# A prologue's opening in another order, its ScalarE loop written out with one table load, and twenty instead of sixteen maximum pairs beside projections

## The reference

```python
x = x + attn(layernorm(x))        # x: 4096 x 256, 16 heads of 16
x = x + ffn_fp8(layernorm(x))     # 256 -> 256, quantised to fp8 values

# attn:
qkv = x @ Wqkv + b                                  # q, k, v by head
y_softmax = softmax(causal(q k^T / 4)) v
state = (1 - sigmoid(Lambda)) * state + Gamma * (v_t outer k_t / 4)   # per token
y_stp = (W_static + state) q_t
alpha = sigmoid(gelu(x @ gate_w1 + b1) @ gate_w2 + b2)
return (alpha * y_softmax + (1 - alpha) * y_stp) @ out_w + out_b
```

## Time and profile before

| | us |
|---|---|
| median of 3 runs (1756.3 to 1759.27) | 1756.9 |
| profiled execution | 1765.1 |
| its span | 1763.3 |
| TensorE busy | 1626.0 |
| VectorE busy | 1520.4 |
| ScalarE busy | 1394.1 |
| GpSimd busy | 1249.5 |

### The profile page before, as it was taken

How to read it: one execution, slowest core, us unless ns; L and a number is a source line. 1 busy time by engine, 2 the same in 40 slices (tenths; PEclk the granted TensorE clock), 3 DMA queues, 4 the chain that set the end, 5 groups by cost and what they waited for, 6 DMA issues and landing times. The chain is left out here.

```text
span 1763.3 us, 44702 instructions
## 1 busy us (share of the span) xinstructions
PE 1626.0 (92%) x17582; PEld 587.1 (33%) x17582; DVE 1520.4 (86%) x1736; ACT 1394.1 (79%) x2839; POOL 1249.5 (71%) x1159
## 2 busy tenths in 40 slices
PE   5996699999999999999999999999999999999655
PEld 3541133223333332333333322333333332333542
DVE  6568899999899999998999999989999999830778
ACT  3652388998987889989888998898888889898234
POOL 4435487778777777787777777877788888870645
PEclk9995599999999999999999999999999999999876
DMA  4885333241222331422124222322252221200702
GB/s 131 272 267 165 80 88 87 73 103 57 74 67 85 101 89 56 96 78 70 59 87 111 68 80 71 83 72 67 77 119 83 78 83 43 79 5 17 254 32 96
DMA packets 115346, 163.22 MB, mean 93 GB/s; under 512 B 30080, under 2 KB 57792, under 8 KB 115136
## 3 DMA queue, kind: packets, MB, share of 16 engines
q1 hardware_dynamic: 112608, 158.74, 30.7%
q10 hardware_dynamic: 2528, 1.64, 0.3%
HBM read 121.87 MB, written 38.01 MB: 91 GB/s over the span
## 5 line engine op out<-in xcount | busy, mean ns | idle before, releaser
L1519 DVE TENSOR_REDUCE pmax<-PS 128x2 f32<-128x1024 f32 (+2 forms) x1120 | 1204.2, 1130 | 85.3 <-PE PS L1318 67.2
L1472 ACT ACTIVATE probs<-PS 128x512 f32<-128x512 f32 (+3 forms) x2304 | 1149.1, 576 | 157.0 <-PE PS L1356 77.9
L1383 PE MATMUL PS<-probs,V_g 128*17 128x256 f32 (+3 forms) x5064 | 395.9, 385 | 4.1 <-ACT o_t L1493 3.7
L1226 POOL TENSOR_TENSOR v_exp<-v_exp,k_rows 128x512 f32<-128x512 f32 x256 | 321.9, 1283 | 28.1 <-DMA v_exp<-qkv_t 27.9
L1356 PE MATMUL PS<-Q_st,K_st 50*128 50x512 f16 (+3 forms) x1408 | 289.1, 365 | 7.9 <-ACT probs L1472 6.3
L1268 POOL TENSOR_TENSOR state<-odd,q_rows 128x514 f32<-128x514 f32 x256 | 281.7, 1132 | 6.1
L1318 PE MATMUL PS<-K_st,Q_st 48*128 48x512 f16 (+3 forms) x1408 | 272.9, 357 | 0.2
L1383 PE MATMUL PS<-probs,V_first 128*17 128x256 f32 (+2 forms) x3296 | 265.3, 394 | 2.2 <-ACT o_t L1493 2.2
L1356 PE MATMUL PS<-Q_st,K_first 50*128 50x512 f16 (+3 forms) x896 | 194.4, 380 | 11.0 <-ACT probs L1472 5.0
L1318 PE MATMUL PS<-K_first,Q_st 48*128 48x512 f16 (+1 forms) x832 | 179.1, 392 | 19.6 <-DVE pmax L1519 19.4
L1257 POOL COPY carry<-odd 128x4 f32<-128x4 f32 x64 | 12.0, 187 | 252.6 <-DVE odd L1554 252.6
(11 more groups left out here) (194 smaller groups left out, 1511.6 us busy)
## 6 DMA issues: line engine op xcount, KB each, us to landing
v_exp<-qkv_t SPq DMA_DIRECT2D x256, 256.0 KB
qkv_t<-proj SPq DMA_DIRECT2D x24, 512.0 KB, 4.1
qk_parts<-parts SPq DMA_DIRECT2D x16, 512.0 KB, 5.2
Q_st<-qk_parts SPq DMA_DIRECT2D x192, 32.0 KB, 3.8
v_rows<-vaug SPq DMA_DIRECT2D x8, 544.0 KB, 6.1
xin<-x SPq DMA_DIRECT2D x8, 512.0 KB, 6.5
k_rows<-qkv_t SPq DMA_DIRECT2D x16, 256.0 KB, 4.0
q_rows<-qkv_t SPq DMA_DIRECT2D x16, 256.0 KB, 6.1
```

Of the source, the lines that this page charges most:

```text
L1226: pool.tensor_tensor(v_exp[:, n % RING], v_exp[:, n % RING], k_rows[:, b % 2], ALU.mult)\
L1383: mm = pe.matmul(PS[h * VW:h * VW + VN, out_bank(g, s), first:end], v[:, kt, h * VN:(h + 1) * VN], probs[:, tile % P_SLOTS, h, first - r * ...
L1472: act.activation(probs[:, tile % P_SLOTS, h, 0:CH - r * P], PS[:, step[5], 0:CH - r * P], ACT.Exp, scale=SCORE_SCALE).then_inc(exp_done, 1)
L1519: dve.tensor_reduce(pmax[:, s % 2, pair * TPC + j:GH * TPC:PAIRS * TPC, blk], PS[:, bank:bank + SIDES, 0:width], AX.X, ALU.max).then_inc(m ...
```

## The change

It has five parts.

1. `PAIRS_AT`: chunk 5 keeps four pairs but starts one unit later, chunk 6 gets seven (six before), chunk 7 nine (six before). A unit may have two pairs behind it; `project` counts them.
2. The ten K_first fills of GpSimd move from behind the second `power` into its loop: four behind the third `power`, four behind the fourth, two behind the fifth.
3. ScalarE's loop is written out for all chunks, and a Gelu of one column stands after the weights. Its output is overwritten later.
4. VectorE's `low_columns(0, 0)` moves ahead of the last steps of the scales.
5. `set_recurrence` becomes three functions. `peak_of_ffn` stays ahead of the loop, `set_decays` (the eight steps up to `gains_ready`) goes behind `split(0, 0)`, `set_static` (`static_j`) behind `low_columns` of the same round.

```diff
-PAIRS_AT = {5: (2, 3, 4, 5), 6: (0, 1, 2, 3, 4, 5), 7: (0, 1, 2, 3, 4, 5)}
+PAIRS_AT = {5: (3, 4, 5, 5), 6: (0, 0, 1, 2, 3, 4, 5), 7: (0, 0, 1, 2, 2, 3, 4, 4, 5)}
...
                     power(2)
-                    for pair in range(PAIRS):
-                        for c in range(FIRST):
-                            pool.memset(K_first[:, pair, c * CH:(c + 1) * CH], SHIFT_UNIT).then_inc(shift_rows_ready, 1)
                     pool.wait_ge(pool_setup, 12)
...
                         power(c1)
+                        for c in range(2 * (c1 - 3), min(2 * (c1 - 2), FIRST)):
+                            for pair in range(PAIRS):
+                                pool.memset(K_first[:, pair, c * CH:(c + 1) * CH], SHIFT_UNIT).then_inc(shift_rows_ready, 1)
...
-                            if u in between:
+                            for _ in range(between.count(u)):
                                 first_maxima(MAX_BANKS[pairs_made % 2], 2 if pairs_made else 1)
...
+                    act.activation(gate_t[:, 0, 0:1], w1_sb[:, 0, 0:1], ACT.Gelu)
...
-                    with act.Fori(0, NCH // 2 - 1) as it:
+                    for it in range(NCH // 2 - 1):
...
                     low_weights(w_parts[:, 1, :, 0:2 * D], wqkv_sb[:, :, 0:2 * D], w_parts[:, 0, :, 0:2 * D], 1)
+                    low_columns(0, 0)
...
-                    low_columns(0, 0)
...
-                    set_recurrence()
+                    peak_of_ffn()
                     for it in range(NCH // 2 - 2):
                         for par in range(2):
                             split(it, par)
+                            if it == 0 and par == 0:
+                                set_decays()
                             low_columns(it + par, 1 - par)
+                            if it == 0 and par == 0:
+                                set_static()
```

More of the change, by code:

```diff
@@ L975, in link, with peak_of_ffn @@
                         dve.wait_ge(dve_setup, n_setup)
-                    def set_recurrence():
+                    def peak_of_ffn():
                         dve.wait_ge(weights_loaded, 16 * N_WEIGHTS)
@@ L983, in set_recurrence, with set_decays @@
                         dve.tensor_copy(ffn_peaks[:, :], wsmall[:, 0:1].broadcast_to([P, P])).then_inc(weights_peak, 1)
+                    def set_decays():
                         dve.wait_ge(act_setup, 1)
@@ L994, in set_recurrence, with set_static @@
                         dve.sem_inc(gains_ready, 1)
+                    def set_static():
                         n_c = HD // TPC
```

## The result

The change makes the kernel faster: median 1748.57 us (1745.2 to 1752.51) against 1757.3 us (1755.73 to 1764.23) of the kernel before, timed in turn; the ratio is 0.9948 with a 95% interval of 0.9937 to 0.996. That is 8.7 us, where 12.5 were forecast; 1748.6 lies inside the range, 4.2 us above the predicted 1744.4.

What follows compares the result with a forecast made beforehand. The prologue was taken to be clocked by TensorE's chunks, its gains passing on whole through block two. Steps 1 to 7 gave -10.0 us and step 8 -2.5, together -12.5 from the median 1756.9: 1744.4, range 1738.5 to 1751.

Steps and rivals of the forecast that it cites:

- block two passing it on whole: Second block, behind a barrier of all engines: whatever the first block gains or loses passes on whole.
- Step 1: Start of chunk 0: low_columns(0,0) ahead of the scales' six small instructions, -1.06 us; chunk 0 keeps its 10.62.
- Step 2: Gap before chunk 1: ten fills leave VectorE's way, chunk 1 starts near 33.6 instead of 39.44, -5.8 us including step 1.
- a clock that isn't regained: Rival: chunks 1 and 3 still begin at half clock, losing 2.4 + 1.7 us, giving 1748.5; chance 0.15.
- Step 3: Chunk 1: idle time gone, so it runs at full clock, 9.27 instead of 11.63 us, -2.4; running sum -8.2.
- Step 4: Before chunk 2: static_j held by low_half(0), then xn held by four fills, +1.0 us; running sum -7.0.
- Step 5: Gap into chunk 3: table load gone, -1.28 us, but VectorE's full round makes TensorE wait, +0.95; running sum -7.1.
- Step 6: Chunks 3 to 5: chunk 3 at full clock -1.7 us, gap 4 to 5 without table load -1.28; chunk 5 at -9.7.
- Step 7: K loads in chunk 5: first pair at 91.1 us after waiting some 1.2, one unit less behind; chunk 5 ends at -10.0.
- Step 8: Chunks 6, 7 and tail: four fewer pairs at the end -4.2 us, their cost beside the chunks +1.75; net -2.5.
- transfers crowd: Rival: chunk 3's stores land 3 us late and the K gate is late by as much, giving 1747.5; chance 0.05.

Runs made afterwards that it cites:

- after: Profiled execution of the whole changed kernel, against the kernel before: span 1746.1 us against 1763.3.
- p_gate_unit3: Block one of the changed kernel alone, chunk 5's pairs placed as in the change but sixteen pairs in all: median 162.0 us (160.8 to 163.77).
- the block alone: Block one of the changed kernel, blocks two and three left out: median 159.75 us, against 166.83 and 171.76 for the two groups of block one of before.
- p_idle_fills: Block one of the changed kernel alone, five fills ahead of the third power and five ahead of the sixth: median 158.2 us, against the change's 159.75.
- after_again: The whole changed kernel once more, unchanged, in another session: 1749.13 us (1747.26 to 1752.72), ratio to before 0.9958.
- one-fill block: Block one of the kernel before alone, its ten K_first fills written as one instruction: 171.37 to 172.69 us in six runs.

## Why the prediction was right, and where not

**What bounds the kernel, and block two passing it on whole.** Right: 1475.03 against 1474.84 us.

**Step 1, low_columns early.** TensorE started chunk 0 at 19.61, 1.37 earlier than 20.98; 0.29 of that is the whole execution being earlier (TensorE's first instruction at 10.69, not 10.98). But chunk 0 took 11.95, not 10.62. Before and the other traces show 10.6 to 12.0 for it, with and without this step, so this is scatter more than a price of the step, and I have no run that explains it; the granted clock is 1.00 over all of chunk 0 in after (11.95) and in p_gate_unit3 (10.68) alike. It did cost something: chunk 1 of after starts behind TensorE's own small groups, 2.75 us after chunk 0 ends and without a wait for VectorE, and in p_gate_unit3, with the same interval, at 33.08 instead of 34.31. At chunk 5 0.6 of that is left (82.62 against 83.22).

**Step 2, the fills.** As a reading of the profiled execution right (xn done at 27.38, forecast 27.9; chunk 1 at 34.31, forecast 33.6). **Here the step failed that carried the error**: "The two engines exclude each other there" was taken as a property of the program, and it is one outcome of a race. What decides the outcome no run shows. In the other outcome the first xn takes 1.04 us, and of the change's gain 5.2 us were already there. By traces the last reduction goes from 155.56 or from 150.37 to 142.31, that is 13.25 or 8.1 us; the block alone gave 12.0 or 7.1, and the medians' 8.7 lies near the lower of each, as it would with most runs of before not held; that they were not is an inference. The sign of it stood in the table of times: the profiled execution was 8.2 us above the median (by now I can place that as 5.2 of hold and 3.5 or so of a longer block three). The sum subtracted 12.5 from both alike. That 1748.6 lies inside the range all the same is luck: no rival names a before that isn't held, and the range reached so far up for a clock that isn't regained (1748.5), which didn't happen.

**Step 3, chunk 1 at full clock.** Right: 9.23 us at 1.00, with no wait of TensorE ahead of it in the timeline. The rival that the clock isn't regained is out. But this too is in before already when it isn't held (9.24 at 36.09).

**Step 4, static_j held.** The mechanism is there: static_j took 2.47 us instead of 1.00: the first of its four instructions lasted from 34.10 to 35.80, low_half(0) ended at 35.73, and the other three took 0.22 each. That also agrees with the rule of the Trainium skill, SBUF — State Buffer, "Who interferes with whom", for an instruction with two SBUF inputs. The four fills held xn (2.94, not 1.38). The size was off: xn ended at 43.61 and chunk 1's matmuls at 43.54, and TensorE went on with the transposes at 43.67, so it lost some 0.1, where +1.0 was charged. low_half(0) began at 31.64 and not at 31.9, and xn was done 0.3 earlier than in the sum, while chunk 1 ended 0.6 later; the term was a difference of two sums, smaller than the error of either.

**Step 5.** Charged 0.95, measured 1.21; p_idle_fills shows that the fills were its whole cause (no wait at 57.92). Chunk 3 at 59.38, forecast 60.05.

**Step 6.** Right: chunk 3 at full clock, chunk 5 at 83.22 (forecast 84.4), -10.9 where -9.7 was forecast. Part of that is a slip: -7.1, -1.7 and -1.28 make -10.1, not -9.7. It didn't carry on, since step 7 goes by the K gate.

**Step 7, the K gate.** Pair at 90.10 (91.1), wait 1.52 (1.2), end of chunk 5 at 95.62 against 106.44, -10.8 (-10.0). What the step missed is how near it stood to a loss: with the old place of the first pair the same loads cost 3.8 us more.

**Step 8, twenty pairs.** In the two profiled executions TensorE's end moved from -10.8 behind chunk 5 to -13.25 behind the last reduction: -2.4, forecast -2.5, and p_gate_unit3 gives 2.2 to 2.3. Behind the two pairs in a row of chunk 6 TensorE waited 0.36 and 0.72 for a reduction (102.06, 104.57), where 0.4 was charged, and in chunk 7 not at all. The step priced only the count of pairs and not that the table moves the first one behind one more unit; beside the earlier chunks of the change that is worth more than the count, 3.8 to 3.9 us.

So the gain divides otherwise than forecast. By the ends of the last reduction, against an execution of before that is not held, the opening and the table load bring 2.0 us (150.37 to 148.38) and the table of pairs 6.1 (148.38 to 142.31). The ratios of the whole kernels, 0.9984 with the old table and 0.9948 with the new, give some 2.8 and 6.3; they are from two sessions, and the interval of each is some 2 us to either side. The forecast had 10 and 2.5. The division holds for this order only, since with the old table the K gate takes back much of what the opening gives; the new table in the kernel before was not run. The rival "transfers crowd" didn't come in the profiled execution: the first early load followed the issue of chunk 3's last store after 5.34 us, in before after 5.32. In after_again it was 6.40, a microsecond late and never the rival's 3.

**Still open:** how often the kernel before is held. In the first session its 17 runs leave a gap of 2.8 us: eight lie at 1753.38 to 1755.98, nine at 1758.82 to 1761.96, their medians 4.6 apart, which is near the 5.2 of the hold. All nine of its runs in the second session lie at 1759.91 or above, 14 of 17 in the third below 1758. But only a trace can tell, and block two's own scatter (1474.6 to 1480.9 us) is as large as the hold, and I have no run that explains that scatter, nor that of chunk 0.

## What to carry to other kernels

An instruction that lasts many times its usual in a profile may be one outcome of a race: before it is priced, see how far the profiled execution lies from the median, and take a second trace. Work that waits for transfers gains nothing from compute that comes sooner; the wait grows, the clock may fall behind it, and a table that says where the first waiting work stands should be moved along with the change. Put an engine's fills where it waits anyway, not where a partner's shortest instructions stand.

## What the runs showed of the hardware

- VectorE's xn behind a row of ten fills of 0.46 us: 6.62 us, or 1.04 with the fills then taking 5.42 instead of 4.72. Behind the same ten written as one instruction of 4.36 us, and sum_e, it took 6.17. I had expected one outcome. Behind rows of four fills both occur too: 2.94 for four xn with the fills taking 1.92, and 2.58 with 2.20.
- Waits of TensorE of 1.38, 1.47, 1.52, 1.58, 2.63 and 2.72 us at the K gate (the last in block one of the change alone) left the unit behind it at 1.47 us; waits of 2.98 and 3.07 were each followed by one of 2.74 at a granted clock of 0.50, the lower of the two levels. The 1.55 us of longer wait thus cost 2.3 more.
- A table load between chunks cost its 1.28 us (the gap was 4.05 with it, 2.69 without), and with it half clock in chunk 3, chunk 5 or both. In before, in its second profile and in block one with the fills moved, chunk 3 took 10.93 us instead of 9.24; in block one of before, chunk 5's first three units took 5.75 instead of 4.06; in the one-fill block and in the whole kernel with the fills moved, both did. In the eight traces without these loads neither did. The slow start of chunk 5 cost little, since it stood where TensorE otherwise waits for the K loads (no wait at the first pair in the three traces that have it).
